# Routing inside the second 8-wide heads, a region of memory for each expert, and tiles read one by one

## The chip, the cores and the metric

The kernel runs on one core of a Trainium2 chip. The metric is the time of one execution in device microseconds, the median of the runs. The core has TensorE (matrix products, 128x128), VectorE and ScalarE (elementwise work), GpSimd (elementwise work, and transfers to rows given by an index), SyncE (SP, which issues the other transfers), an on-chip SBUF of 128 partitions, and eight PSUM banks. Engines run their own instruction streams in order and meet at semaphores.

## The reference, cut to what matters

Tokens are 32 sequences of 128, width 128, float32. Four layers follow each other, each an attention and a feed-forward part, both on a layer norm of `x` and added to `x`:

```python
x = x + _L2_xattn_ref(_layernorm(x), ctx, ctx, mask, ...)   # 16 heads of 8
x = x + _L2_ffn_ref(_layernorm(x), centroid, Wg, bg, W1, b1, W2, b2)
# _L2_ffn_ref, E = 8, K = 2, D = 128, H = 342
d2 = sum(xs * xs) + sum(centroid * centroid) - 2.0 * (xs @ centroid.T)
dist = sqrt(maximum(d2, 1e-12))
w, sel = top_k(dist, K)
w = softmax(w)
for e in range(E):
    h = silu(xs @ Wg[e] + bg[e]) * (xs @ W1[e] + b1[e])
    out = out + we[:, e:e + 1] * (h @ W2[e] + b2[e])
```

So each of the 4096 tokens goes to two of eight experts, 8192 rows in all. Layers 0, 1 and 3 are as they were.

## The kernel before

The program is a list of phases (attention and feed-forward of each layer). Each phase gives a function for each engine, and `barrier` at its end makes every engine wait for all five. The two phases here are `small_heads(2, ...)` (L280 on; the same maker also builds layer 0's heads) and `gated_experts` (L1707 on).

**small_heads.** B = 32 batches in NG = 8 groups of G = 4. A slot n = 4g + j is the attention of one batch, and in each slot TensorE makes scores of batch n+2, the turned scores and exponents' input of batch n (`turned`), and the values' product of batch n-1 (`attend`). The tile of scores `pair` holds half of the heads, so that VectorE takes two maxima a slot: `maximum(n+2, 0)`, then `normalise(n-1)`, then `maximum(n+2, 1)` and `split_max`. TensorE's `mask_scores` waits for a maximum to have read `pair`, and `turn_max` for `split_max`. Beside this, one PSUM bank M is used in turn by the group's other work: in slot j = 0 the queries of group g+1 (`project_q`), in j = 1 its values, in j = 2 the output of group g-1 (after which VectorE adds the residual and takes statistics), in j = 3 the transposes of group g+2 (`turn`) and at the slot's end its keys (`project_k`, copied by ScalarE's `evac_k`, its last instruction of the slot). VectorE's `moments(g-1)` is in slot 3 too. GpSimd runs a loop over g: for g >= 2 `residual(g)` (adds a constant row to x), then `rstd_of` group g-2 once `stats_ready` allows, then `masked(g+2)`, four multiplications that wait for the keys of group g+2. After the loop come the last two rstd. SyncE loads the context of each group, two groups ahead, once the values two groups back are made.

**gated_experts.** VectorE normalises all rows to `xn`; TensorE turns them and makes the distances' logits; VectorE chooses two experts per token for all 32 batches at once (`first_best` twice), TensorE counts with a triangular and a full matrix of ones, VectorE sums the counts over batches, and adds for each expert a base of full tiles: expert e's rows begin at a multiple of 128 behind those of the experts ahead. `where_i` holds each token's two rows. GpSimd scatters (L2100): for each batch and choice one indirect transfer of 128 rows of 130 words (128 values, the token's number, a code of the first choice) into the memory table `tokens_by_tile` of 72 tiles of 128 rows, which SyncE has filled with blanks (L1772, 8 transfers). When all 64 have landed, SyncE loads the 72 tiles in 8 transfers of 9 tiles (L1777). Then the tile loop: transpose (L1824), gate and up products (L1832, L1838), ScalarE copies the expert's weights (L1882) and applies the gate (L1889), VectorE multiplies (L2036) and copies (L2028, L2045), TensorE makes the down product (L1849) and GpSimd scatters the result (L2110). `places` on VectorE works out where the rows of 9 tiles go. SyncE reads the results back, ScalarE weighs them, and they are added to x.

## Time and profile before

| | us |
|---|---|
| median of 3 runs | 2105.51 |
| lowest and highest | 2103.83, 2106.74 |
| profiled execution | 2106.39 |
| span of its profile | 2104.5 |
| TensorE busy | 1760.6 (84%) |
| VectorE busy | 1061.4 (50%) |
| ScalarE busy | 912.2 (43%) |
| GpSimd busy | 665.5 (32%) |

The busy time is a sum over the whole span; a stage's own limit is read from a stretch of it. The second 8-wide heads run from about 920 to 1206 us from the span's start, the experts of layer 2 from there to about 1527. The profile counts waiting and the issue of transfers by SyncE as not busy.

### The profile page before, as it was taken

The page shows a single profiled execution, that of the slowest core. Times are in us where ns is not written, and L with a number is a line of the kernel's source. Part 1 is how long each engine was busy: PE and PEld are TensorE (multiplying, and loading weights), DVE is VectorE, ACT ScalarE, POOL GpSimd, SP SyncE. Part 2 cuts the span into 40 slices and gives each one's busy share as a digit, 9 for nine tenths or more (in the row PEclk, how much of TensorE's full clock was granted, in tenths as well). Part 3 has the DMA queues.
Part 4 walks back from the last instruction along what each step waited for, and adds up shares of the span by engine and source line. Part 5 has one row for each costly group of instructions (what it writes and reads, how often), then busy time and mean ns, then how long its engine had stood idle before and what let it go on. Part 6 is the DMA issues. An engine that isn't in the chain of part 4 may idle for free.

```text
span 2104.5 us, 47728 instructions
## 1 busy us (share of the span) xinstructions
PE 1760.6 (84%) x18872; PEld 1265.5 (60%) x18872; DVE 1061.4 (50%) x2947; ACT 912.2 (43%) x2497; POOL 665.5 (32%) x664
## 2 busy tenths in 40 slices
PE   6999984788489999979999740599369999999988
PEld 3555573666457877855565440599336666666763
DVE  4666546676432211234665540366635555555558
ACT  2333320676144444423333210377626566556635
POOL 3323202676211111121223117455612333332315
PEclk8999976888589999988999955799779999999979
DMA  5000001000000000020000021411310000000001
GB/s 168 7 13 7 2 2 25 16 11 1 6 1 2 2 2 1 1 94 14 8 12 3 17 89 52 121 32 32 90 57 6 1 7 6 6 6 1 2 1 41
DMA packets 45785, 50.76 MB, mean 24 GB/s; under 512 B 6858, under 2 KB 36453, under 8 KB 45309
## 3 DMA queue, kind: packets, MB, share of 16 engines
q1 hardware_dynamic: 41213, 39.19, 6.2%
q0 software_dynamic: 4352, 8.47, 1.3%
q8 instruction: 159, 2.61, 0.5%
q14 instruction: 61, 0.50, 0.1%
HBM read 32.29 MB, written 15.87 MB: 23 GB/s over the span
## 4 chain that ended last, share of the span: by engine, by line
PE 56%; issue 13%; DVE 5%; POOLq 4%; POOL 3%; DMA 1%; SPq 1%; ACT 1%; DVEq 1%; ACTq 0%
PE single L1520 5%; PE quad L1508 5%; PE pair L394 3%; PE single L445 3%; PE quad L1832 2%; PE single L1849 2%; PE quad L1838 2%; PE quad L422 2%; PE pair L2273 2%; PE pair L1467 2%; PE quad L2273 2%; PE single L2285 2%; PE quad L2250 1%; PE quad L2299 1%; PE single L2257 1%
## 5 line engine op out<-in xcount | busy, mean ns | idle before, releaser
L568 DVE TENSOR_REDUCE arena<-pair 128x8 f32<-128x1024 f32 x128 | 156.7, 1224 | 149.3 <-PE pair L394 146.9
L2506 POOL TENSOR_TENSOR arena<-arena 128x512 f32<-128x512 f32 x128 | 130.4, 1040 | 312.4 <-DVE arena L2429 312.4
L655 POOL TENSOR_SCALAR arena<-arena 128x512 f32<-128x512 f32 x56 | 86.7, 1565 | 307.8 <-ACT arena L500 307.8
L251 POOL TENSOR_TENSOR rstd<-var_eps,neg_half 128x4 f32<-128x4 f32 (+1 forms) x64 | 68.2, 1066 | 336.4 <-DVE var_eps L247 242.8
L548 ACT ACTIVATE arena<-quad 128x1024 f32<-128x1024 f32 x128 | 124.1, 1022 | 71.1 <-PE quad L428 71.1
L1578 ACT ACTIVATE arena<-quad,arena 128x256 f32<-128x256 f32 x256 | 110.7, 475 | 100.4 <-PE quad L1508 100.3
L394 PE MATMUL pair<-arena 32*128 32x512 f32 x512 | 147.3, 652 | 0.0
L2366 ACT ACTIVATE arena<-pair,arena 128x128 f32<-128x128 f32 x256 | 90.9, 380 | 91.4 <-DVE arena L2424 91.4
L1661 DVE TENSOR_TENSOR arena<-single,arena 128x512 f32<-128x512 f32 x32 | 22.1, 691 | 212.8 <-PE single L1520 212.8
L1508 PE MATMUL quad<-arena,wide 128*128 128x256 f32 x512 | 121.7, 385 | 4.7 <-issue 3.9
L1520 PE MATMUL single<-wide,arena 128*64 128x128 f32 x2048 | 123.9, 275 | 0.0
L2366 ACT ACTIVATE arena<-quad,arena 128x128 f32<-128x128 f32 x256 | 90.9, 381 | 75.9 <-DVE arena L2424 75.9
L1520 PEld LDWEIGHTS single<-wide,arena 128*64 128x64 f32 x2048 | 110.7, 137 | 15.9 <-issue 11.0
L1889 ACT ACTIVATE arena<-quad,arena 114x128 f32<-114x128 f32 x216 | 63.5, 364 | 119.3 <-PE quad L1832 118.1
L1508 PEld LDWEIGHTS quad<-arena,wide 128*128 128x128 f32 x512 | 93.3, 190 | 20.8 <-issue 8.7
L2110 POOL DMA_INDIRECT outputs_by_choice<-arena x72 | 71.0, 986 | 79.9 <-DVE arena L2045 65.2
L2036 DVE SCALAR_TENSOR_TENSOR arena<-quad,arena 114x128 f32<-114x128 f32 x216 | 62.4, 344 | 54.0 <-ACT arena L1889 43.1
L1824 PE MATMUL pair<-ident,arena 128*128 128x128 f32 x72 | 20.0, 281 | 82.9 <-DMA arena<-tokens_by_tile 82.9
L584 DVE RECIPROCAL arena<-single 128x128 f32<-128x128 f32 x64 | 61.3, 958 | 51.4 <-PE single L445 51.4
L1688 POOL TENSOR_TENSOR arena<-arena 128x512 f32<-128x512 f32 x32 | 34.8, 1097 | 164.8 <-DVE arena L1642 160.3
L445 PEld LDWEIGHTS single<-arena 128*32 128x32 f32 x2048 | 52.1, 109 | 48.4 <-issue 46.8
L2100 POOL DMA_INDIRECT tokens_by_tile<-arena x64 | 62.0, 969 | 59.3 <-DVEq L2002 40.1
(475 smaller groups left out, 4379.8 us busy)
## 6 DMA issues: line engine op xcount, KB each, us to landing
arena<-in_ctxT SPq DMA_DIRECT2D x32, 256.0 KB, 2.8
tokens_by_tile<-arena SPq DMA_DIRECT2D x8, 585.0 KB, 6.9
arena<-tokens_by_tile SPq DMA_DIRECT2D x8, 585.0 KB, 8.1
wide<-in_w SPq DMA_DIRECT2D x2, 2048.0 KB, 10.0
arena<-outputs_by_choice SPq DMA_DIRECT2D x16, 256.0 KB, 5.7
wide<-in_wgu SPq DMA_DIRECT2D x1, 2736.0 KB
x<-in_x SPq DMA_DIRECT2D x4, 512.0 KB, 7.2
out_x<-x SPq DMA_DIRECT2D x8, 256.0 KB, 2.3
```

Of the source, the lines that this page charges most:

```text
L394: mm = pe.matmul(S[:, r * 512:(r + 1) * 512], qT[g % 2][rows, j * P:(j + 1) * P], kv[g % 2][rows, j, :, :].rearrange("p a k -> p (a k)"), ...
L445: mm = pe.matmul(O[strip(c), k * P:(k + 1) * P], lhs(h), probs[m % 2][:, h, :], start=(a == 0), stop=(a == 3), skip_group_check=True)
L548: act.activation(probs[n % 2][:, 8 * p:8 * p + 8, :].rearrange("p h q -> p (h q)"), T[:, 1024 * p:1024 * p + 1024], ACT.Exp).then_inc(s["s ...
L568: dve.tensor_reduce(mx[m % 2][:, 8 * p:8 * p + 8], S[:].rearrange("p (h k) -> p h k", h=8), AX.X, ALU.max).then_inc(s["s_free"], 1)
L655: mm = pool.tensor_scalar(kv[g % 2][:, :, a, :], kf[g % 2], kmask[:, a:a + 1], None, ALU.mult)
L1508: pe.matmul(bank[2 + f][:, 0:G * K], w1[:, e, f * P:(f + 1) * P], exT[u][:, e, :], start=True, stop=True).then_inc(s["h_ready"], 1)
L1520: mm = pe.matmul(bank[6 + pair % 2][K * r:K * r + K, j * P:(j + 1) * P], h1T[e % 4][:, f, j * K:(j + 1) * K], w2[:, e, f, :], start=(f == ...
L1578: act.activation(h1T[e % 4][:, f, :], bank[2 + f][:, 0:G * K], ACT.Gelu_apprx_tanh, bias=b1c[:, e, f:f + 1]).then_inc(s["h_evac"], 1)
L2110: pool.indirect_dma_start(done, bass.IndirectOffsetOnAxis(ap=back_i[:, n:n + 1], axis=0), ysb[n % SLOTS], None, bounds_check=2 * B * P - 1 ...
L2273: mm = pe.matmul(S[o][:, r * 512 + i * P:r * 512 + (i + 1) * P], qT[g % 2][rows, 4 * o + i, j * P:(j + 1) * P], kT[g % 2][rows, 4 * o + i, ...
L2366: mm = act.activation(probs[t % 3][:, i, :], S[t % 2][:, i * P:(i + 1) * P], ACT.Exp, bias=minus_max[t % 3][:, i:i + 1], accum_out=total[t ...
L2506: pool.tensor_tensor(part, part, inv[t % 3][:, 4 * r:4 * r + 4].unsqueeze(2).broadcast_to([P, 4, P]), ALU.mult).then_inc(s["norm_ready"], 1)
```

## The change

Routing is done in units of two groups (UNIT = 8 batches). Units 0, 1 and 2 (batches 0 to 23) are routed inside `small_heads(2)`, unit 3 at the start of `gated_experts`.

In the heads: VectorE makes the normal rows of group g-1 in slot 3 of group g (`rows_normal`); TensorE turns them at the start of slot 0 of the next group (`turn_rows`, in bank M) and makes the logits behind `attend`, in an unused part of bank O; in the slots of groups 3, 5 and 7 VectorE chooses, sums and finds rows (`route`), with the count products behind `attend` in slot 2. `project_q` moves behind `attend` in slot 0. GpSimd builds the tables at its start, and scatters unit 0 in its pass g = 5, unit 1 in g = 7, unit 2 after its last rstd.

In memory each expert has a region of 4096 rows of its own (`tokens_by_expert`, 33,792 rows), so that a token's row no longer depends on how many tokens other experts get. The blanks, now 22 transfers of 12 x 128 rows, are written during the heads. In the experts a tile's first row is worked out on VectorE (`start_i`), read into a register by SyncE and loaded by a transfer of its own, up to eight ahead of the loop; `places` works on 4 tiles.

```diff
@@ program
-        fw_loads = {0: 3, 1: 3 + 1 + E + 1, 2: 1 + 2 + 1 + 1, 3: 2}
+        fw_loads = {0: 4, 1: 3 + 1 + E + 1, 2: 2 + 1 + 1, 3: 2}
...
+        REGION = B * P
+        FILL, FILLS = 12, (E * REGION + E * P) // (12 * P)
+        UNIT = 2 * G
+        by_tile = nc.dram_tensor("tokens_by_expert", [E * REGION + E * P, ROW], F32).ap()
...
+        def first_best(dve, values, chosen, top):
+            dve.tensor_reduce(top, values, AX.X, ALU.max)
+            dve.drain()
+            dve.tensor_tensor(key, values, along(top), ALU.is_equal)
...
+        def scatter(pool, k):
+            for n in range(k * UNIT, k * UNIT + UNIT):
+                for i in range(2):
+                    pool.indirect_dma_start(by_tile, bass.IndirectOffsetOnAxis(ap=where_i[:, i, n:n + 1], axis=0),
+                                            xr[:, n, :], None).then_inc(routed, 16)
@@ small_heads, sync
                 for g in range(2, NG):
                     load_ctx(sp, g)
+                    if l == 2 and g < 6:
+                        if g == 2:
+                            sp.wait_ge(blanked, 1)
+                        for i in range((g - 2) * 6, min((g - 1) * 6, FILLS)):
+                            sp.dma_start(by_tile[i * FILL * P:(i + 1) * FILL * P].rearrange("(p r) d -> p (r d)", p=P),
+                                         blank.rearrange("p r d -> p (r d)")).then_inc(blanked, 16)
@@ small_heads, tensor
+                def turn_rows(g):
+
+                    pe.wait_ge(s["xr_ready"], g + 1)
+                    pe.wait_ge(s["k_evac"], min(g + 4, NG))
+                    pe.wait_ge(s["x_done"], g + 1)
+                    for j in range(G):
+                        mm = pe.transpose(M[:, j * P:(j + 1) * P], xr[:, g * G + j, 0:P], ident[:])
+                    mm.then_inc(s["rt_ready"], 1)
...
+                    at, slot = divmod(m + 1, G)
+                    if routes(at) and at < NG and slot == 0:
+                        mm = logits(at - 2)
+                    if routes(at) and at % 2 == 1 and slot == 2:
+                        mm = counts((at - 3) // 2)
                     mm.then_inc(s["pv_ready"], 1)
...
-                    if j == 0 and g + 1 < NG:
+                    if j == 0 and routes(g):
+                        turn_rows(g - 2)
+                    if j == 0 and g + 1 < NG and l == 0:
                         project_q(g + 1, M)
...
                         attend(n - 1)
+                    if j == 0 and g + 1 < NG and l == 2:
+                        project_q(g + 1, M)
@@ small_heads, vector
+                def route(k, slot):
+                    if slot == 0:
+                        dve.drain()
+                        choose_first(dve, k)
+                    elif slot == 1:
+                        choose_second(dve, k).then_inc(s["sel_ready"], 1)
+                    elif slot == 2:
+                        sum_blocks(dve)
+                    else:
+                        find_rows(dve, k).then_inc(s["rows_ready"], 1)
+
+                def rows_normal(g):
+                    dve.wait_ge(s["rstd_ready"], g + 1)
+                    normal_rows(dve, g).then_inc(s["xr_ready"], 1)
...
                     if n + 2 < N:
                         maximum(n + 2, 0)
+                    if j == 3 and 1 <= g < NG - 1 and l == 2:
+                        rows_normal(g - 1)
                     if n >= 1:
                         normalise(n - 1)
                     if n + 2 < N:
                         maximum(n + 2, 1)
                         split_max(n + 2)
+                    if routes(g) and g % 2 == 1:
+                        route((g - 3) // 2, j)
@@ small_heads, gpsimd
                     if g >= 2:
                         residual(g)
                         pool.wait_ge(s["stats_ready"], g - 1)
-                        rstd_of(pool, (g - 2) * G)
+                        mm = rstd_of(pool, (g - 2) * G)
+                        if l == 2:
+                            mm.then_inc(s["rstd_ready"], 1)
                     if g + 2 < NG:
                         masked(g + 2)
+                    if l == 2 and g in (5, 7):
+                        pool.wait_ge(s["rows_ready"], (g - 3) // 2)
+                        if g == 5:
+                            pool.wait_ge(blanked, 1 + 16 * FILLS)
+                        scatter(pool, (g - 5) // 2)
                 for g in (NG - 2, NG - 1):
                     pool.wait_ge(s["stats_ready"], g + 1)
                     rstd_of(pool, g * G)
+                if l == 2:
+                    pool.wait_ge(s["rows_ready"], 3)
+                    scatter(pool, 2)
                 barrier(pool, phase)
@@ gated_experts, sync
-                sp.wait_ge(s["scattered"], 16 * 2 * B)
-                for i in range(LOADS):
-                    part = slice(i * PART, (i + 1) * PART)
-                    sp.dma_start(tokens[:, part, :], by_tile[i * PART * P:(i + 1) * PART * P]
-                                 .rearrange("(r p) d -> p r d", p=P)).then_inc(s[f"landed{i}"], 16)
+                sp.wait_ge(s["starts_ready"], 1)
+                sp.wait_ge(routed, 16 * 2 * B)
+                for n in range(TILES):
+                    if n >= LANES:
+                        sp.wait_ge(s["y_copied"], n - LANES + 1)
+                    row = sp.value_load(start_i[0:1, n:n + 1], min_val=0, max_val=E * REGION + E * P - P)
+                    sp.dma_start(tokens[:, n, :], by_tile[ds(row, P)]).then_inc(s[f"tile_in{n % LANES}"], 16)
@@ gated_experts, vector
-                for g in range(NG):
-                    for j in range(G):
-                        n = g * G + j
-                        mm = dve.tensor_scalar(xn[:, n, 0:P], x[:, n, :], mean[:, n:n + 1], rstd[:, n:n + 1],
-                                               ALU.subtract, ALU.mult)
-                    mm.then_inc(s["xn_ready"], 1)
-
+                for g in range(2):
+                    normal_rows(dve, 2 * K + g).then_inc(s["xr_ready"], 1)
...
+                choose_first(dve, K)
+                choose_second(dve, K).then_inc(s["sel_ready"], 1)
+                dve.wait_ge(s["counts_ready"], 1)
+                copy_counts(dve, count_bank)
+                sum_blocks(dve)
+                find_rows(dve, K).then_inc(s["rows_ready"], 1)
@@ gated_experts, gpsimd
-                pool.wait_ge(s["slots_ready"], 1)
-                pool.wait_ge(s["zeroed"], 1 + 16 * 8)
-                for n in range(B):
-                    for i in range(2):
-                        pool.indirect_dma_start(by_tile, bass.IndirectOffsetOnAxis(ap=where_i[:, i, n:n + 1], axis=0),
-                                                xn[:, n, :], None).then_inc(s["scattered"], 16)
+                pool.wait_ge(s["rows_ready"], 1)
+                scatter(pool, K)
```

`choose_first` has ten small operations (128x64 or 128x8), `choose_second` seven, `sum_blocks` eight, `find_rows` eight; `scatter` sixteen transfers.

## Rows read from the trace of the kernel before

**Rows 1.** Windows by stage: busy us (instructions), TensorE's clock, DMA share, GB/s.

```profile
920.00:1206.00 286.00, 261.69 (x4578) 154.83 (x4578) 163.97 (x332) 92.95 (x130) 66.33 (x49) 0.94 0.07 24
1206.00:1337.40 131.40, 25.16 (x114) 23.77 (x114) 25.80 (x90) 8.41 (x14) 65.33 (x76) 0.50 0.22 76
1337.40:1495.00 157.60, 154.65 (x1368) 153.26 (x1368) 96.65 (x388) 112.22 (x288) 83.83 (x80) 0.98 0.20 54
```

**Rows 2.** Timeline of GpSimd in the heads: start, duration, instruction, [idle before <-releaser].

```profile
1021.99 1.04 POOL L251 TENSOR_TENSOR rstd<-var_eps,neg_half 128x4 f32<-128x4 f32 x1
...
1109.25 6.19 POOL L655 TENSOR_SCALAR arena<-arena 128x512 f32<-128x512 f32 x4 [23.13 <-ACT arena L500]
...
1116.64 1.04 POOL L251 TENSOR_TENSOR rstd<-var_eps,neg_half 128x4 f32<-128x4 f32 x1
...
1166.93 1.02 POOL L251 TENSOR_TENSOR rstd<-var_eps,neg_half 128x4 f32<-128x4 f32 x1 [6.49 <-DVE var_eps L603]
...
1204.95 1.01 POOL L251 TENSOR_TENSOR rstd<-var_eps,neg_half 128x4 f32<-128x4 f32 x1 [9.37 <-DVE var_eps L603]
```

**Rows 3.** Timeline of VectorE, slots 1 to 3 of group 4.

```profile
1087.71 1.11 DVE L562 TENSOR_SCALAR arena<-x,mean,rstd 128x128 f32<-128x128 f32 x4
1090.36 1.22 DVE L568 TENSOR_REDUCE arena<-pair 128x8 f32<-128x1024 f32 x1 [1.54 <-PE pair L394]
...
1097.95 1.23 DVE L568 TENSOR_REDUCE arena<-pair 128x8 f32<-128x1024 f32 x1 [0.98 <-PE pair L394]
...
1103.60 0.16 DVE L603 TENSOR_SCALAR var_eps<-arena 128x4 f32<-128x4 f32 x1
1105.54 1.23 DVE L568 TENSOR_REDUCE arena<-pair 128x8 f32<-128x1024 f32 x1 [1.78 <-PE pair L394]
1107.44 0.96 DVE L584 RECIPROCAL arena<-single 128x128 f32<-128x128 f32 x1 [0.68 <-PE single L445]
...
1109.88 1.23 DVE L568 TENSOR_REDUCE arena<-pair 128x8 f32<-128x1024 f32 x1 [1.11 <-PE pair L394]
```

**Rows 4.** Timeline of TensorE: weight loads of an output, and a projection of queries.

```profile
1093.53 0.97 PEld L379 LDWEIGHTS single<-wo,arena 128*128 128x128 f32 x8 [0.76 <-issue]
...
1109.76 1.12 PE L361 MATMUL single<-arena,wq 128*128 128x512 f32 x2
```

**Rows 5.** Windows of 1 us for the clock, and two slots' ends on VectorE.

```profile
1203.00:1204.00 1.00, 0.00 (x0) 0.00 (x0) 0.91 (x5) 0.00 (x0) 0.00 (x0) 0.71 0.00 0
...
1343.00:1344.00 1.00, 1.00 (x9) 1.00 (x9) 0.10 (x1) 0.87 (x4) 0.00 (x0) 0.82 1.20 295
...
957.49 0.18 DVE L578 SCALAR_TENSOR_TENSOR arena<-arena 128x16 bf16<-128x16 f32 x1
...
967.40 0.18 DVE L578 SCALAR_TENSOR_TENSOR arena<-arena 128x16 bf16<-128x16 f32 x1
```

**Rows 6.** Timeline of the experts' front, all engines, and one scatter of results.

```profile
1206.04 9.07 DVE L1913 TENSOR_SCALAR arena<-x,mean,rstd 128x128 f32<-128x128 f32 x32 [1.17 <-POOLq L121]
...
1207.49 8.65 SPq L1772 DMA_DIRECT2D tokens_by_tile<-arena  x8
...
1215.21 1.71 PE L1805 MATMUL quad<-gate,arena 128*128 128x8 f32 x8
...
1216.78 1.09 PE L1792 MATMUL pair<-ident,arena 128*128 128x128 f32 x4
...
1242.65 0.20 DVE L1967 COPY arena<-arena 128x64 f32<-128x64 f32 x1
...
1250.02 1.67 POOL L2100 DMA_INDIRECT tokens_by_tile<-arena  x1 [40.11 <-DVEq L2002]
...
1330.25 0.96 POOL L2100 DMA_INDIRECT tokens_by_tile<-arena  x1 [0.30 <-issue]
1333.11 14.04 SPq L1777 DMA_DIRECT2D arena<-tokens_by_tile  x8
...
1345.76 0.99 POOL L2110 DMA_INDIRECT outputs_by_choice<-arena  x1 [14.55 <-DVE arena L2045]
```

357 lines of the change are left out of this document (216 added, 141 removed).

## The prediction

> **What bounds the kernel now.** I read first the busy time by stage [rows 1]. In the second 8-wide heads (920 to 1206) TensorE is busy 261.7 of 286 us at a granted clock of 0.94: a stage with almost no room. In the routing front of the experts (1206 to 1337.4) TensorE is busy 25 of 131.4 us and nothing is really computing: this is what the change attacks. In the tile loop (1337.4 to 1495) TensorE is busy 154.7 of 157.6 us, 2.19 us a tile for 72 tiles. Then I read the front as a timeline [rows 6]: normalised rows, transposes and logits, a choice on VectorE, and from 1250.02 to 1331.2 GpSimd issuing 64 scatters, one each 1.27 us, with nobody able to do anything useful. Last I read the heads' boundary between two groups on GpSimd [rows 2], VectorE [rows 3] and TensorE [rows 4], because the change puts new waits there.
>
> **Part 1, the front gets shorter.** Only the last unit of eight tiles is routed here. From the start of the stage (T): eight normal tiles at 9.07/32 = 0.28 us, the first four ready at T+1.2; transposes of a group 1.09 and its logits 1.71, all at the low clock as now [rows 6]. In TensorE's order (turn, turn, logits, logits), with ScalarE's copies beside it, that is done at T+2.3, 3.4, 5.2 and 6.9. VectorE then has 2 distance operations, 17 of the choice, the copy of the counts, 8 of the block sums and about 7 of the rows. A 128x64 operation takes 0.20 us and its successor starts some 0.08 later [rows 6]; with 0.28 a step, and pairs that overlap, distances and choice take 5.3, the count matmuls 1.1, the rest 3.6: rows known at T+17. Sixteen scatters at the spacing of [rows 6], (1330.25 - 1250.02)/63 = 1.27: 15 x 1.27 + 0.96 = 20.1, with 0.7 more for the slow first one: T+38. From the last scatter's end to the first reading transfer it takes 1.9 us now (1331.2 to 1333.11) and the first 585 KB block is usable 4.3 us later [rows 1, 6]; a tile of 65 KB behind a register read should take 2 to 4, I take 3: first tile at T+43. Against 131.4: **-88** (bounds -82 to -92). The tables of tile starts lie under the scatters.
>
> **Part 2, a scatter tail on the heads.** The third unit's rows are ready before the heads end, but GpSimd issues its 16 scatters after the last rstd. That rstd runs at 1204.95 to 1205.96 and the stage ends 0.08 later [rows 2, 6]. Now 20.1 to 20.8 us of scatters stand between, and all engines wait at the barrier: **+21** (20 to 23). Nothing hides it.
>
> **Part 3, the wait that decides.** VectorE gets in slot j = 3 of group g, for g = 1 to 6, between the first and the second maximum, `rows_normal(g-1)`, which waits for the rstd of group g-1. The statistics for it are ready early (1103.60 in [rows 3]). But GpSimd computes that rstd only in its pass g+1, behind `masked(g+2)`, and that waits for the keys that ScalarE copies at the very end of the same slot. In the trace it goes so [rows 2, 3]: the first maximum of the slot ends at 1106.77; masked starts at 1109.25 and takes 6.19; the rstd runs 1116.64 to 1117.68. Today nobody waits for it (there are five of this kind, the first at 1021.99). After the change VectorE stands from 1106.8 to 1117.7, then makes the four rows (1.11, as L562 in [rows 3]), the normalisation that it did from 1107.44 to about 1108.8 (1.35), and only then the second maximum (1.23), which ended at 1111.11: it will end at about 1121.5. TensorE's next score masks and the turned maxima wait for exactly this, and so does its new `turn_rows`. So each boundary gets 10.4 us longer, for g = 1 to 5: 52 us (9 to 11 each). For g = 6 there is no masked left and the rstd follows the statistics (as at 1166.93), so there it costs under 1 us.
> At g = 5 there is more: the first unit's 16 scatters are put behind masked(7) and ahead of pass 6, where the rstd is that VectorE wants. Queued behind them are residual(6) and this rstd; VectorE waits, and TensorE and ScalarE for it. +20.1 to 20.8. The second unit's scatters (pass 7) hold back only an rstd that no engine of the stage wants. **Together +73** (65 to 77).
>
> **Part 4, work inside the heads.** (a) project_q moves from the start of slot 0, where TensorE waits for the second maximum anyway, to behind attend: 1.12 [rows 4], now in the open, 7 times: +7.7 (5 to 8). `turn_rows` takes its old place in the shadow: nothing; if that cover is gone, 0.7 each. (b) Logits: 4 matmuls of 8 columns are bound by their weight loads, 0.97 for eight loads [rows 4], for 6 groups: +5.7 (4 to 7). Counts: 4 loads each, 3 times: +1.4. (c) VectorE: choose_first 10 x 0.28 = 2.8 against an idle time of 1.54 ahead of the next first maximum, choose_second 2.0 against 0.98 [rows 3]; of the excess about half a microsecond is hidden because TensorE needs that maximum later. About 1 us per odd group, three of them: +3 (0 to 8). Sums and rows fit in the longer idle times. (d) The setup (tables, row numbers, blank) lies beside the first loads: 0 (to +2).
> (e) The blank fill grows from 8 x 585 KB to 22 x 799 KB, 17.6 MB. The 8 old ones were issued in 8.65 us [rows 6] and landed at most some 8 us after, 4.7 MB in 17 us; six new ones are 4.8 MB in each group of 31.6 us. A context load is queued behind one batch and is needed more than a group (31.6 us) later: 0.
>
> **Part 5, the clock.** The clock of TensorE follows its work: when the heads' last matmuls are done it falls from 2.4 to 1.2 GHz (0.71 in 1203 to 1204, [rows 5]), and after the restart at 1337.4 it rises only in 1343 to 1344. At the start of the heads, where it is low for most of the time, a slot lasts from 957.49 to 967.40 [rows 5], 9.9 us, instead of the 7.6 from one first maximum to the next [rows 3]. Each of the five stalls has some 9 us without a matmul, so each should be followed by one slot at the low clock: 5 x 2.5 = **+12** (3 to 25). TensorE: Matmul & The Clock Gate (What's actually happening, in the Trainium skill) says the throttled state is the default and activity releases it; the rows agree. If a stall of this kind left the clock up, the sum would be 12 less.
>
> **Part 6, the tile loop.** 72 single loads, each behind a register read, eight in flight. The 8 big loads took 14.04 us in all [rows 6], 0.2 us a tile if it is descriptors, 1.8 a load if it is by instruction: both below 2.19, so the queue keeps up. `places` every 4 tiles instead of every 9 is 10 more rounds of 0.75 us on an engine with a third of its time free: 0 (to +6).
>
> **Sum.** -88 + 21 + 73 + 7.7 + 5.7 + 1.4 + 3 + 12 = +36. The profiled execution took 2106.4 (span 2104.5 and 1.9 outside), 0.9 above the median of 2105.5: 2106.4 + 36 = 2142. All terms at their low ends give about +5, at their high ends +70.
>
> **Rivals.**
> 1. The wait costs little, because VectorE's and GpSimd's order overlap other than I read, or TensorE's buffers cover it. Then Part 3 and Part 5 fall away and the time is 2106.4 - 88 + 21 + 18 = 2057, faster. For it speaks that the front's 88 us are sure; against it that the two maxima and the rstd are in strict order on their engines, and that TensorE has a depth of one slot only. The deciding point: from about 2.5 us per boundary (plus the scatters) upward the change is no longer faster than 1%; at 3 us less per boundary than I say it is still slower. Chance 0.12.
> 2. The wait costs half: if attend and the keys shift earlier within the slot, or the g = 5 scatters find the needed rstd done. 2142 - 36 = 2106, within a few us of no change. Chance 0.06.
> 3. The 72 loads do not keep up, since a load with a register's row costs the queue 2.5 us or more: 72 x 0.4 = +29 on my sum, 2171. No row shows such a load. Chance 0.08.
> 4. Scatters are slowed by VectorE's work beside them. In this trace a scatter beside a busy VectorE in the tile loop takes as long to issue as in the quiet front (0.99 against 0.96, [rows 6]). As a mechanism here: the second unit's scatters begin after 1168 in old time [rows 2] and have 38 us before the last rstd, 2.4 us each; were each issued in three times its 0.96, with the 0.3 between, they would take 51 and push the tail out by 13: 2155. SBUF — State Buffer (Who interferes with whom, in the Trainium skill) has it that GpSimd is shut out of writing descriptors while VectorE runs a two-port operation; that is the rule behind this rival, and the row of the tile loop speaks against its size here. Chance 0.04.
> 5. The forecast: both waits as computed. Chance 0.70, with 2125 to 2170 as its own range.
>
> **Numbers.** A measurement can tell about 0.2% (4 us) from no change. Faster: rival 1 and a third of rival 2: 0.14. Within 0.2%: 0.03. Slower: 0.83. The range reaches from 2104, the low ends of all terms and half of rival 2, to 2176, the high ends and rival 3.
>
> **What would show it.** In the profile after: VectorE idle about 11 us ahead of the new row operation in slot 3, released by GpSimd's rstd, four times, and 31 us once; TensorE idle 9 us at the same places, its clock at 0.5 after them; sixteen scatters of 20 us between the last rstd and the next stage; 43 us from there to the first tile's transpose; an unchanged 157 us for the tiles. The heads' stage, 286 us now, should take about 286 + 103 + 21 = 410. What would make the prediction wrong: less than 370 there (the wait is not what I read), or more than 165 for the tiles.

## The result, and the profile after

The changed kernel took 2178.1 us (median of 4, 2175.4 to 2179.8) against 2105.0 of the kernel before beside it: ratio 1.0346, interval 1.0328 to 1.0364. The prediction had the side right (slower) and the size wrong: +73 us, not +36, and 2 us outside its range. One thing from the experiments belongs here: on another chip the same kernel took 2140.2 us (e5), 2 us from the predicted 2142, and on a third 2168.6 (e9). The kernel before took 2101 to 2105 on all of them.

Windows of the profile after, in the order heads, scatter tail, front, tile loop (to be held against [rows 1]):

```profile
921.20:1329.30 408.10, 303.34 (x4664) 181.00 (x4664) 183.40 (x457) 96.63 (x137) 99.95 (x87) 0.81 0.18 65
...
1329.30:1353.50 24.20, 0.00 (x0) 0.00 (x0) 0.01 (x1) 0.00 (x0) 15.44 (x16) 0.50 0.13 44
1353.50:1395.40 41.90, 9.09 (x40) 8.23 (x40) 15.05 (x65) 4.44 (x6) 17.58 (x22) 0.50 0.09 28
1395.40:1562.00 166.60, 157.45 (x1368) 153.58 (x1368) 100.87 (x414) 111.08 (x287) 82.67 (x78) 0.98 0.21 56
```

The front is 42 us in place of 131, the tail 24. The heads are at 408 in place of 286, at a mean clock of 0.81 in place of 0.94. The tile loop is 9 us longer.

VectorE in the heads, every instruction of it that stood long (timeline; the bracket is the idle time before it and who ended it):

```profile
1024.76 1.12 DVE L327 TENSOR_SCALAR arena<-x,mean,rstd 128x128 f32<-128x128 f32 x4 [10.93 <-POOL rstd L262]
...
1069.91 1.11 DVE L327 TENSOR_SCALAR arena<-x,mean,rstd 128x128 f32<-128x128 f32 x4 [10.94 <-POOL rstd L262]
...
1115.99 1.11 DVE L327 TENSOR_SCALAR arena<-x,mean,rstd 128x128 f32<-128x128 f32 x4 [10.90 <-POOL rstd L262]
...
1163.21 1.12 DVE L327 TENSOR_SCALAR arena<-x,mean,rstd 128x128 f32<-128x128 f32 x4 [10.94 <-POOL rstd L262]
...
1232.81 1.12 DVE L327 TENSOR_SCALAR arena<-x,mean,rstd 128x128 f32<-128x128 f32 x4 [31.43 <-POOL rstd L262]
...
1287.46 0.96 DVE L782 RECIPROCAL arena<-single 128x128 f32<-128x128 f32 x1 [19.35 <-remote]
```

The first five are the waits of Part 3, four of 10.9 us and one of 31.4: they end at exactly the rstd that [rows 2] showed behind masked. The sixth was not foreseen. VectorE waits there for pv_ready, which is TensorE's, but the profile finds no TensorE instruction that ends then and says "remote". What GpSimd, TensorE and ScalarE did at that time:

```profile
1264.17 1.02 POOL L262 TENSOR_TENSOR rstd<-var_eps,neg_half 128x4 f32<-128x4 f32 x1 [6.48 <-DVE var_eps L822]
...
1265.37 1.03 POOL L415 DMA_INDIRECT tokens_by_expert<-arena  x1 [0.18 <-issue]
...
1271.51 3.12 PE L568 MATMUL pair<-arena 32*128 32x512 f32 x4
...
1284.43 0.96 POOL L415 DMA_INDIRECT tokens_by_expert<-arena  x1 [0.31 <-issue]
...
1288.29 0.60 ACT L711 ACTIVATE arena<-single 128x512 f32<-128x512 f32 x1 [21.40 <-remote]
...
1289.97 0.63 PE L155 MATMUL pair<-maskS2own,identb 64*64 64x512 bf16 x1 [11.78 <-DVE arena L766]
```

From 1265.37 to 1285.39 GpSimd issues the 16 scatters of scatter(1), which no engine of the stage waits for. Four matmuls of L568 last 3.12 us instead of 1.08, and TensorE's signals reach VectorE and ScalarE only 2 us after the last scatter. The products that VectorE waits for (L619) are on record until 1270.1, 17 us before it goes on. From about 1278 TensorE itself waits, for the maximum that VectorE can only take after that. So the halt, as I call it, has two parts: TensorE's instructions come slowly, and their signals come late.

### The profile page after: what moved, and what is told of

Read it like the earlier page. It is cut to its first block, busy times and chain, and to the rows that moved or that the text cites. A ratio compares the mean times of both kernels' runs of the same rounds, so it can differ in the third digit from the quotient of the medians.

```text
span 2178.1 us, 48570 instructions
## 1 busy us (share of the span) xinstructions
PE 1791.6 (82%) x18884; PEld 1276.6 (59%) x18884; DVE 1077.5 (49%) x3087; ACT 911.6 (42%) x2496; POOL 666.3 (31%) x664
## 4 chain that ended last, share of the span: by engine, by line
PE 54%; issue 10%; DVE 7%; POOL 6%; POOLq 4%; DVEq 2%; DMA 1%; ACT 1%; another core or an unknown queue 1%; SPq 1%; ACTq 0%
PE single L1778 5%; PE quad L1766 5%; PE single L2076 2%; PE quad L2059 2%; PE quad L2065 2%; PE pair L568 2%; PE single L619 2%; PE pair L2434 2%; POOL tokens_by_expert L415 2%; PE pair L1725 2%; PE quad L2434 2%; PE single L2446 2%; POOLq L132 1%; PE quad L2411 1%; PE quad L596 1%
## 5 line engine op out<-in xcount | busy, mean ns | idle before, releaser
L568 PE MATMUL pair<-arena 32*128 32x512 f32 x512 | 153.5, 673 | 0.0
L619 PEld LDWEIGHTS single<-arena 128*32 128x32 f32 x2048 | 53.8, 112 | 51.8 <-issue 43.1
L596 PE MATMUL quad<-arena 32*128 32x128 f32 x2048 | 83.3, 304 | 0.0
L715 ACT ACTIVATE arena<-single 128x128 bf16<-128x128 bf16 x64 | 17.8, 278 | 154.9 <-PE single L580 154.9
```

What stands on the lines that cost most here:

```text
L568: mm = pe.matmul(S[:, r * 512:(r + 1) * 512], qT[g % 2][rows, j * P:(j + 1) * P], kv[g % 2][rows, j, :, :].rearrange("p a k -> p (a k)"), ...
L596: pe.matmul(T[:, r * 512 + a * P:r * 512 + (a + 1) * P], kv[g % 2][strip(r), j, a, :], qT[g % 2][strip(r), j * P:(j + 1) * P], start=False ...
L619: mm = pe.matmul(O[strip(c), k * P:(k + 1) * P], lhs(h), probs[m % 2][:, h, :], start=(a == 0), stop=(a == 3), skip_group_check=True)
```

## Experiments

The runs fell on four chips, called W, X, Y and Z here; that of the first measurement isn't recorded. Runs that are compared stood on the same chip unless it is said.

**e1 (chip W): the wait alone taken away.** In the second heads GpSimd's order is changed, nothing else:

```diff
-                    if g >= 2:
+                    if g >= 2 and l == 0:
                         residual(g)
                         pool.wait_ge(s["stats_ready"], g - 1)
-                        mm = rstd_of(pool, (g - 2) * G)
-                        if l == 2:
-                            mm.then_inc(s["rstd_ready"], 1)
+                        rstd_of(pool, (g - 2) * G)
+                    if 1 <= g < NG - 1 and l == 2:
+                        residual(g + 1)
+                        pool.wait_ge(s["stats_ready"], g)
+                        rstd_of(pool, (g - 1) * G).then_inc(s["rstd_ready"], 1)
                     if g + 2 < NG:
                         masked(g + 2)
```

> The changed kernel with one edit: in the second 8-wide heads GpSimd runs residual(g + 1) and rstd(g - 1) before masked(g + 2), not behind it. Everything else is computed as before. Theory of the wait (the prediction's): the five waits of VectorE for rstd of 10.9 us each and the sixth of 31.4 us go, since rstd(g - 1) needs only the statistics of the same slot; 54.7 + 31.4 = 86 us leave the stage and some of TensorE's clock comes back, so 2085 to 2095 us. Rival (a scatter halts TensorE by itself): scatter(1) stood beside TensorE's work for 19 to 21 us in the changed kernel without being waited for. Then scatter(0), which now also runs beside TensorE's work, costs its 20 us again, and the time is 2105 to 2115 us. In both the group periods of groups 2 to 4 fall from 45 to 47 us to 33 to 36 us.

Measured: 2064.0 us, ratio to the kernel before 0.9811 (0.9777 to 0.9845). The wait is gone; of e1 the rstd on GpSimd, and the rows on VectorE right behind the first maximum:

```profile
1045.40 1.04 POOL L262 TENSOR_TENSOR rstd<-var_eps,neg_half 128x4 f32<-128x4 f32 x1 [6.47 <-DVE var_eps L822]
```

```profile
1047.10 1.23 DVE L766 TENSOR_REDUCE arena<-pair 128x8 f32<-128x1024 f32 x1 [1.78 <-PE pair L568]
1048.24 1.11 DVE L327 TENSOR_SCALAR arena<-x,mean,rstd 128x128 f32<-128x128 f32 x4
```

It is 21 us below the low end of what I expected, and both bursts of scatters ran beside TensorE's work (1160.67 to 1180.85 and 1184.55 to 1204.53) with no halt. So either the halt needed the wait, or it hung on something outside the program. The expectation was counted from the 2178 of another chip; e5 shows what it should have been counted from.

**e2, e3 (chip W): scatters alone.** The kernel before with 16 scatters of its own behind masked(6), and with plain transfers of the same bytes in their place:

```diff
+                    if l == 2 and g == 4:
+                        for i in range(16):
+                            pool.indirect_dma_start(extra_rows, bass.IndirectOffsetOnAxis(ap=extra_at[:, i:i + 1],
+                                                    axis=0), extra, None).then_inc(extra_done, 16)
```

```diff
+                            pool.dma_start(extra_rows[i * P:(i + 1) * P], extra).then_inc(extra_done, 16)
```

> The kernel before with 16 indirect scatters added in the second 8-wide heads, on GpSimd right behind masked(6), one behind the other: each writes a blank tile of 128 rows of 520 bytes to a DRAM tensor of its own, at row numbers set at the start. Nothing reads it and GpSimd has no consumer that is late by its 20 us there. If scatters only cost the time of GpSimd: no change, 2105 us within 3. If a burst of scatters halts TensorE by itself: 15 to 21 us more, 2120 to 2126 us, with VectorE waiting for TensorE in one stretch of the burst's length.

> As the previous one, with 16 plain transfers from GpSimd's queue in the place of the indirect scatters: same tile, same bytes. If it is the bytes or the queue that halts TensorE, the time rises as there (15 to 21 us); if it is the indirect form, in which GpSimd works out the descriptors, it stays at 2105 us within 3.

Measured: 2103.0 (0.9996, 0.9980 to 1.0011) and 2104.8 (0.9996, 0.9980 to 1.0012), ten runs each: nothing, on this chip.

**e5, e6, e7, e8 (chip X).** e5 is the changed kernel untouched.

> The changed kernel, unchanged, on the chip of the other runs of this call. Asked: is the halt of 19 us at scatter(1) (VectorE and ScalarE waiting for semaphores of TensorE that came only when the last scatter had landed), and the hitch at every eighth tile of the tile loop, in this kernel's every run, or in some executions or chips only? If it belongs to the kernel: 2178 us within 5, with a wait of about 19 us ahead of RECIPROCAL and a tile loop of 161 us between first and last transpose. If it belongs to the chip or the execution: without the halt and with a tile loop of 149 us, 2140 to 2150 us.

Measured: 2140.2 (2137.3 to 2143.4), ratio 1.0175 (1.0140 to 1.0210). Its five waits are there (10.92, 10.94, 10.89, 10.93 and 31.37), the halt isn't. Windows of e5: the heads, the 23 us at scatter(1), tail, front, tile loop:

```profile
919.00:1300.30 381.30, 293.07 (x4664) 175.36 (x4664) 187.72 (x457) 96.63 (x137) 99.14 (x87) 0.83 0.19 70
1259.70:1282.90 23.20, 21.71 (x419) 13.35 (x411) 15.38 (x35) 6.97 (x9) 16.39 (x17) 1.00 0.16 49
1300.30:1324.50 24.20, 0.00 (x0) 0.00 (x0) 0.05 (x1) 0.00 (x0) 15.38 (x16) 0.50 0.13 44
1324.50:1366.30 41.80, 9.09 (x40) 8.23 (x40) 14.99 (x65) 4.44 (x6) 17.54 (x22) 0.50 0.09 28
1366.30:1522.00 155.70, 153.95 (x1368) 153.31 (x1368) 100.67 (x417) 112.15 (x288) 83.29 (x79) 0.98 0.22 60
```

and the same 23 us behind rstd(5) in the profile after:

```profile
1264.20:1287.40 23.20, 11.34 (x124) 5.06 (x116) 2.25 (x5) 1.94 (x2) 16.44 (x17) 0.65 0.14 48
```

GpSimd did the same (16.4 us in 17 instructions), the transfers moved the same (49 GB/s in e5, 48 in the profile after). TensorE began 419 matmuls in e5 and 124 in the profile after.

e6 moves scatter(0) only:

```diff
-                    if l == 2 and g in (5, 7):
-                        pool.wait_ge(s["rows_ready"], (g - 3) // 2)
-                        if g == 5:
+                    if l == 2 and g in (6, 7):
+                        pool.wait_ge(s["rows_ready"], g - 5)
+                        if g == 6:
                             pool.wait_ge(blanked, 1 + 16 * FILLS)
-                        scatter(pool, (g - 5) // 2)
+                        scatter(pool, g - 6)
```

> The changed kernel with scatter(0) moved from behind masked(7) to behind rstd(4), one step of GpSimd's order later; nothing else differs, so the five waits of 10.9 us stay. Theory of the wait: the wait of 31.4 us in group 5 becomes one of 10.9 like the others, so 20 to 21 us less than the changed kernel run beside it. Rival (a burst of scatters beside TensorE's work halts it): the 20 us come back as a halt during scatter(0), and the time is that of the changed kernel within 4 us.

Measured: 2123.7 (1.0088, 1.0054 to 1.0121), 16.5 less than e5, where 20 to 21 were expected; the fifth wait is like the others:

```profile
1214.61 1.12 DVE L327 TENSOR_SCALAR arena<-x,mean,rstd 128x128 f32<-128x128 f32 x4 [10.93 <-POOL rstd L262]
```

The heads are 22.2 us shorter (table below). So a scatter(0) behind which nobody is queued costs nothing on this chip, and ahead of the rstd it costs its whole length.

e7 is e1 with the third unit's scatters out of the tail:

```diff
-                if l == 2:
-                    pool.wait_ge(s["rows_ready"], 3)
-                    scatter(pool, 2)
...
+                scatter(pool, 2)
                 pool.wait_ge(s["rows_ready"], 1)
                 scatter(pool, K)
```

> The changed kernel with rstd(g - 1) ahead of masked(g + 2), as in e1, and scatter(2) moved from the stage's tail to the start of the experts' stage, in which GpSimd otherwise has nothing to do until the rows of the last unit are known, 16.6 us after the stage begins. The tail of 20 us goes, and scatter(2) + scatter(3) end at 2 x 20.2 us + some 2 us behind the stage's start, not at 16.6 + 20.2: 20 - 5 = 15 to 17 us less than e1's 2064, so 2046 to 2050 us. Rival: VectorE's small operations of the front are slowed by GpSimd's scatters beside them, so that the rows come later than 20 us behind the start: a gain of 10 us or less, 2054 or more.

Measured: 2044.1, ratio 0.9709 (0.9676 to 0.9741), 2 us below what was expected. Tail and front together are one window of 50.1 us, where e5 has 24.2 + 41.8:

```profile
1224.40:1274.50 50.10, 9.09 (x40) 8.23 (x40) 15.43 (x65) 4.44 (x6) 32.45 (x38) 0.50 0.14 44
```

e8 is the kernel before with project_q and its evacuation behind attend:

```diff
-                    if j == 0 and g + 1 < NG:
+                    if j == 0 and g + 1 < NG and l == 0:
                         project_q(g + 1, M)
...
                         attend(n - 1)
+                    if j == 0 and g + 1 < NG and l == 2:
+                        project_q(g + 1, M)
```

> The kernel before with one part of the change alone: in the second 8-wide heads project_q(g + 1) and its evacuation stand behind attend, not at the slot's start. My prediction gave this 7.7 us in all (7 groups x 1.1 us), because its eviction then stands where TensorE has to wait for it. If it is so: 2111 to 2113 us. Rival (ScalarE and the bank are free anyway): no change, 2105 within 3.

Measured: 2109.0, ratio 1.0021 (1.0003 to 1.0039), 6 us above the kernel before beside it by the medians and 4 by the ratio: between the two times expected. The trace is sharper. From one masked to the next on GpSimd, in e8:

```profile
1047.14 6.19 POOL L659 TENSOR_SCALAR arena<-arena 128x512 f32<-128x512 f32 x4 [24.18 <-ACT arena L502]
...
1079.75 6.19 POOL L659 TENSOR_SCALAR arena<-arena 128x512 f32<-128x512 f32 x4 [24.17 <-ACT arena L502]
```

32.61 us a group, against 31.55 in the kernel before (1077.70 to 1109.25, the second in [rows 2]): 1.06 us for each of 7 projections, 7.4.

**e9, e10, e11 (chip Y): the same programs again.**

> The changed kernel, unchanged, once more, on a chip that may be another one. It took 2178 us where it was first measured and 2140 us beside e6 to e8; the 38 us between them are the halts of TensorE beside bursts of scatters (22 us at scatter(1), 12 us in the tile loop). If the halts hang on the chip, this is near one of the two, 2140 or 2178, within 4 us in all of its runs; if they hang on the execution, its runs spread between the two.

> The kernel of e7, unchanged (rstd ahead, scatter(2) in the experts' front), beside the changed kernel. Without halts 2044 us as in e7. With them, if every burst beside TensorE's work halts it: scatter(0) and scatter(1) cost 20 us each and the tile loop 12, so 2095 us; if only what the changed kernel does at scatter(1) brings it about, 2056 us (the tile loop alone).

> The kernel of e2, unchanged (the kernel before with 16 scatters of its own beside TensorE's work), beside the changed kernel. On a chip without halts: 2105 us, as in e2. Where the changed kernel shows the halt: 2120 to 2126 us if a burst of scatters is enough for it, 2105 us if it needs something of the changed kernel.

Measured: the changed kernel 2168.6 (1.0312, 1.0290 to 1.0334), e7's kernel 2088.4 (0.9929, 0.9906 to 0.9952), the kernel before with 16 scatters 2121.9 (two runs, 1.0100, 1.0080 to 1.0121). The first lies between the two expected values, 9 us under the 2178 of the first chip, with 162.1 us of tiles instead of 168.6; the second is 7 under the 2095 of a halt at both bursts. The runs of the changed kernel lie together on each chip (2175 to 2180, 2137 to 2143, 2162 to 2169), so the halt isn't drawn anew at each execution. This chip has it, and in the heads a burst of scatters is all that the kernel before needs to show it: +21 us, where e2, byte for byte the same program, showed nothing. Of e11, TensorE in the burst:

```profile
1112.64 1.25 POOL L701 DMA_INDIRECT extra_rows<-arena  x1 [0.19 <-issue]
...
1118.15 0.51 PE L432 MATMUL quad<-arena 32*128 32x128 bf16 x8
...
1119.82 0.26 PE L432 MATMUL quad<-arena 32*128 32x128 bf16 x4 [1.15 <-issue]
...
1130.47 0.37 PE L449 MATMUL single<-arena 128*32 128x128 f32 x1 [1.04 <-issue]
...
1131.86 0.96 POOL L701 DMA_INDIRECT extra_rows<-arena  x1 [0.31 <-issue]
...
1135.44 1.94 ACT L552 ACTIVATE arena<-quad 128x1024 f32<-128x1024 f32 x2 [17.90 <-remote]
1135.50 1.23 DVE L572 TENSOR_REDUCE arena<-pair 128x8 f32<-128x1024 f32 x1 [17.53 <-remote]
```

and of e2 the same instructions in the same burst:

```profile
1121.11 0.40 PE L432 MATMUL quad<-arena 32*128 32x128 bf16 x16
...
1121.72 1.94 ACT L552 ACTIVATE arena<-quad 128x1024 f32<-128x1024 f32 x2 [1.21 <-PE quad L432]
1122.35 0.81 PEld L449 LDWEIGHTS single<-arena 128*32 128x32 f32 x32 [0.76 <-issue]
```

In e11 TensorE gets through one to four matmuls and then waits for "issue", that is for nothing that the profile shows; the 16 matmuls of L432 that took 0.40 us in e2 are spread over more than 3 us. GpSimd issues one scatter each 1.26 us in both. TensorE doesn't wait for VectorE or ScalarE there; they wait for it, for signals that come 11 to 14 us after the products on record (L432 until 1121.5, L398 until 1124.8). SBUF — State Buffer (Who interferes with whom, in the Trainium skill) says that "PE and ACT never wait on anyone" and that only the port pair of VectorE and GpSimd is contended. e2 agrees, e11 doesn't: its 17.5 us decide for that chip. Whether TensorE waits for SBUF there or for something else, no run shows.

Small bursts halt too. In the tile loop root() (L2267) holds GpSimd for 1.7 us at every eighth tile, after which three result scatters follow each other. The profile after:

```profile
1487.91 1.04 POOL L2271 DMA_INDIRECT outputs_by_choice<-arena  x1 [0.18 <-issue]
...
1489.26 0.99 POOL L2271 DMA_INDIRECT outputs_by_choice<-arena  x1 [0.30 <-issue]
...
1490.55 0.98 POOL L2271 DMA_INDIRECT outputs_by_choice<-arena  x1 [0.30 <-issue]
...
1492.33 0.88 ACT L2112 ACTIVATE arena<-quad,arena 114x128 f32<-114x128 f32 x3 [2.76 <-PE quad L2059]
```

and e5, on chip X:

```profile
1489.02 0.99 POOL L2271 DMA_INDIRECT outputs_by_choice<-arena  x1 [0.30 <-issue]
...
1490.31 0.98 POOL L2271 DMA_INDIRECT outputs_by_choice<-arena  x1 [0.30 <-issue]
...
1491.64 0.88 ACT L2112 ACTIVATE arena<-quad,arena 114x128 f32<-114x128 f32 x3 [0.55 <-PE quad L2059]
```

Same burst, ScalarE's idle time 2.76 against 0.55. In the profile after, seven such pairs of tiles take about 5.9 us instead of 4.2, 12 us in all.

**Stages side by side**, us, from the timelines (heads: ScalarE's first instruction of the stage to the start of the last rstd; then to the first tile's transpose; then to the last result scatter):

```
                        heads   to tile 1   tiles   median of the run
before                  282.4     132.5     157.3   2105.0  (first chip)
after                   405.9      67.2     168.6   2178.1  (first chip)
e16, before + burst     277.1     133.2     155.6   2102.5  (X)
e5, changed             379.9      67.1     156.2   2140.2  (X)
e6, scatter(0) later    357.7      67.3     155.9   2123.7  (X)
e7, both edits          298.8      51.2     156.3   2044.1  (X)
e2, before + burst      277.9     133.1     156.0   2103.0  (W)
e1, rstd ahead          296.1      67.5     155.7   2064.0  (W)
e11, before + burst     295.2     133.1     156.7   2121.9  (Y)
e9, changed             405.7      67.1     162.1   2168.6  (Y)
e10, e7's kernel        341.5      52.3     162.6   2088.4  (Y)
```

The first slots of the heads differ by up to 5 us from run to run (277.1 to 282.6 for unchanged heads), so a difference of that size in the first column says nothing. The later slots repeat closely: from one RECIPROCAL of VectorE to the next a slot of the unchanged heads takes 7.59 us, or 8.8 at the end of a group, in e3, e12 and e16 alike. Where few us matter I go by slots below.

**e4 (chip W): pairs, in the wrong place.** e7's kernel, but with the scatters of units 0 and 1 two at a time, one pair in each slot of groups 4 to 7:

```diff
+                        for j in range(G):
+                            if g >= 4:
+                                pool.wait_ge(s["pv_ready"], g * G + j)
+                                scatter_one(pool, (g - 4) * G + j)
+                            if j == 2 and 1 <= g < NG - 1:
+                                residual(g + 1)
```

> The changed kernel with rstd(g - 1) ahead of masked(g + 2), as in e1, the scatters of units 0 and 1 issued two at a time, one pair in each slot of groups 4 to 7 (GpSimd waits for the slot's pv_ready), and those of unit 2 moved from the stage's tail into the start of the experts' stage, where GpSimd has 16 us of idle time. Theory of the wait with scatters that cost nothing while GpSimd is on time: 2178 - 86 (waits) - 20 (the halt at scatter(1)) - 17 (tail) - some clock = 2050 to 2060 us, faster than the kernel before. Rival (each scatter halts TensorE for its own 1.27 us, paced or not): 32 x 1.27 = 40 us stay in the stage, 2090 to 2100 us.

Measured: 2071.8 (0.9844, 0.9813 to 0.9874): neither of the two. In slot 3 the pair's own wait for pv_ready stands ahead of the rstd:

```profile
1119.38 2.53 DVE L327 TENSOR_SCALAR arena<-x,mean,rstd 128x128 f32<-128x128 f32 x4 [4.28 <-POOL rstd L262]
```

It is the mistake of the changed kernel in small: 4.3 us of wait, and rows that take 2.53 instead of 1.11 (e1), where GpSimd's masked (from 1119.34) now runs beside them. SBUF — State Buffer (Who interferes with whom, in the Trainium skill) has the port pair that VectorE and GpSimd share as an exclusive lock. That would explain the second; no run here takes it apart.

**e12 to e15 (chip Z), e16 to e18 (chip X): what of the burst does it.** e12 and e17 are e3's kernel, e16 is e2's. e13 issues e2's 16 scatters singly, each behind its own wait:

```diff
+                    if l == 2 and g in (5, 6):
+                        for i in range((g - 5) * 8, (g - 4) * 8):
+                            pool.wait_ge(s["s_ready"], 45 + i)
```

e14 and e15 are e7 with singles and with pairs, both with the slot's rstd first and with root() in sixteen smaller pieces (`n % 4 == 2`); e18 is e15 again. Of e15 (e14 waits for `s_ready` ahead of each scatter instead):

```diff
+                            if j == 3 and 1 <= g < NG - 1:
+                                pool.wait_ge(s["stats_ready"], g)
+                                rstd_of(pool, (g - 1) * G).then_inc(s["rstd_ready"], 1)
+                            if g >= 4:
+                                pool.wait_ge(s["pv_ready"], g * G + j)
+                                for i in range(2):
+                                    scatter_one(pool, (g - 4) * G + j, i)
```

> The kernel of e3, unchanged: the kernel before with 16 plain transfers from GpSimd's queue behind masked(6). On a chip with halts, 16 indirect scatters there cost 21 us (e11). If the bytes or the queue do it: 2117 us or more. If it is the indirect form: 2101 us within 4. On a chip without halts it tells nothing new (2105).

> The kernel before with the 16 indirect scatters of e2 and e11, but spaced: eight in each of two groups, each behind its own wait for s_ready, some 4 us apart, so that one has landed before the next is issued. If the halt comes of scatters that follow each other without a gap: 2101 us within 4 also on a chip with halts. If each scatter halts TensorE for its own time: 2117 us or more, as in e11.

> The changed kernel with rstd(g - 1) ahead of masked(g + 2), scatter(2) in the experts' front as in e7, the scatters of units 0 and 1 issued singly (each behind its own s_ready, some 4 us apart, from group 4 to 7) and behind rstd in slot 3, and root() in sixteen pieces of 4 columns in place of eight of 8, so that no burst of y scatters follows it. If spacing removes the halt: 2040 to 2050 us on any chip (e7's 2044 without halts, 2088 with). If not: 2044 and 2088 to 2095 us. If the scatters put ahead of GpSimd's other work make rstd late as in e4: 2055 to 2065 us.

> As e14 with the scatters in pairs, one pair in each slot behind pv_ready. If a gap of 5 us behind each pair is enough: the time of e14 within 4 us. If the second scatter of each pair halts TensorE for its 1.3 us on a chip with halts: 16 x 1.3 = 20 us more than e14.

> The kernel of e2 and e11 (16 indirect scatters without a gap, in the kernel before), as a control: 2121 us if this chip halts, 2104 within 4 if it doesn't.

> The kernel of e3 and e12 (16 plain transfers of the same bytes from GpSimd's queue). If the indirect form is what halts: 2104 us within 4 also where e16 is at 2121. If the bytes or the queue are: e16's time within 4.

> The kernel of e15 (rstd ahead, scatter(2) in the experts' front, units 0 and 1 in pairs, one pair a slot behind pv_ready, smaller root pieces). If pairs escape the halt: 2045 to 2055 us on any chip, where e7's bursts took 2044 without and 2088 with halts. If they only escaped because the chip of e15 had none: 2065 us or more where e16 is at 2121.

Measured on Z: e12 2106.2 (1.0019, 1.0001 to 1.0038), e13 2111.0 (1.0035, 1.0016 to 1.0054), e14 2058.9 (0.9788, 0.9745 to 0.9830), e15 2052.2 (0.9752, 0.9718 to 0.9787). Measured on X: e16 2102.5 (1.0004), e17 2103.8 (1.0005), e18 2042.1 (0.9715, 0.9686 to 0.9745).

X has no halt, as the control e16 shows, so e17 says nothing of its cause. Z has it, and the traces of Z show it in three places.

First, the tile loop has its hitches (in e12 tiles of 2.59, 2.81 and 2.35 us, as in e11; on X none over 2.3 but two at the start). Second, the experts' front of e14 and e15 has a burst of 32 scatters, of units 2 and 3. Of e15 there, VectorE and ScalarE:

```profile
1256.94 0.76 DVE L2176 TENSOR_TENSOR arena<-arena 128x576 f32<-128x576 f32 x1 [2.58 <-issue]
...
1276.59 0.53 ACT L2106 ACTIVATE arena<-quad 114x432 f32<-114x432 f32 x1 [42.47 <-remote]
```

and of e18, the same program on X, the same ScalarE instruction:

```profile
1251.99 0.53 ACT L2106 ACTIVATE arena<-quad 114x432 f32<-114x432 f32 x1 [22.46 <-PE quad L2051]
```

So the halt is not TensorE's alone. A row of small operations of VectorE (L2171 to L2192 of e15) takes 5.1 us from first start to last in e18 and e7 on X, 15.6 in e15 and 12.6 in e14 on Z, and 11.4 in e10 on Y, with idle times for "issue" in between. It costs little there, since the tiles wait for the scatters anyway. Third, the last five scatters of e14's heads follow each other without a gap, because the value that they wait for is capped, and there TensorE halts:

```profile
1216.63 0.33 PE L605 MATMUL quad<-arena 32*128 32x128 bf16 x9
...
1218.96 0.96 POOL L413 DMA_INDIRECT tokens_by_expert<-arena  x1 [0.30 <-issue]
...
1221.08 0.26 PE L605 MATMUL quad<-arena 32*128 32x128 bf16 x1 [1.19 <-issue]
```

That slot takes 13.7 us from one RECIPROCAL to the next, where e15 has 7.25.

With that, e12 and e15 have an answer, for Z. The plain transfers of e12 leave the heads as they were (277.9, the same as e3 on W), and the slots beside them stay at 7.59 us; its median is 4 us above the kernel before by the ratio, not 17 or more:

```profile
1109.29 8.84 POOL L701 DMA_DIRECT2D extra_rows<-arena  x16
...
1114.45 0.40 PE L432 MATMUL quad<-arena 32*128 32x128 bf16 x16
```

They go through the same queue (software_dynamic), with the same 512 packets and 1.07 MB as the 16 scatters of e11. So on Z neither the queue nor the packets nor the bytes are enough; what is left is the indirect form. (The plain ones are issued in 8.8 us instead of 20; but e14's halt stands beside five scatters in 6 us.) And pairs escape (the time is 7 us below e14's, where it was expected within 4): the heads of e15 take 298.2 us with 16 pairs in them, those of e18 on X 299.0, while the burst in e15's own front halts. The smaller pieces of root() don't escape altogether: they leave five tiles of 2.4 to 2.5 us in e15, and its tiles take 158.8 against 155.6 in e18.

Singles are less clear. The heads of e13 take 286.4 us against 277.9 in e12, and its slots say where: 4.8 of the 8.4 us are one slot, in which a VectorE operation (L580) takes 1.22 us instead of 0.17 beside GpSimd's residual and TensorE's granted clock is then 0.50 (1174 to 1183). That is no halt, and no wait in these heads ends with "remote". The other slots beside scatters are longer by 0.1 to 0.9, and why is open. e14's time lies in the third of its ranges, but not by that range's mechanism: its heads take 311.0, the end of the burst above costs 6.5 of the 12.8 more than e15, and no VectorE wait for rstd is among them. Neither e13 nor e14 ran on a chip without halts.

## Why the prediction was wrong, and where it was right

**Where there is no halt it held, by its own terms.** On chip X (e5 against e16): heads +102.8, predicted 73 + 7.7 + 5.7 + 1.4 + 3 + 12 = 102.8; tail and front -66.1, predicted -88 + 21 = -67; tiles +0.6, predicted 0. Sum +37.3; the medians differ by 37.4 (2140.2 - 2102.8, the kernel before beside e5). To the tenth this is chance: e16's first slots were among the short ones. By slots, from the fourth on, the heads of e5 are 97.6 longer than those of e12, and nearly all of the 5 between is the first slots.
- Part 1: 41.8 to 41.9 us from the stage's start to the first tile, predicted 43. Right.
- Part 2: 24.2, predicted 21. The 16 scatters took 20.0 us (1329.45 to 1349.46); behind them GpSimd stood another 4.1 at the barrier, where in the kernel before the next stage began 0.1 behind the rstd [rows 2, 6]. Low by 3.
- Part 3: four waits of 10.9 and one of 31.4, 75.1 us in the profile after, predicted 73. I counted five waits of 10.4 and added the scatter to the fifth, which is what happened. e1 and e7 show that they are the cause: the heads fall by 81.1 us (e5 to e7), waits and lost clock together, predicted 85. With that rivals 1 and 2 are out.
- Part 4: what is left of the heads without the waits is e7 - e16 = +21.7 us (e1 - e2: +18.2; by slots, e7 against e12, 16.2), predicted 17.8. project_q alone is 7.4 by the group's length in e8, predicted 7.7.
- Part 5: the slots right behind the five waits take 9.9, 9.6, 12.1, 12.4 and 10.2 us in e5, and 9.5, 9.5, 9.3, 9.5 and 9.5 in e7, without waits: 6.9 us, predicted 12. Too high by 5: behind the first two waits it is 0.4 and 0.1, not 2.5, though the granted clock was 0.50 behind the first (e5, 1020.8 to 1027).
- Part 6: the loads keep up; rival 3 is out (156.2 in e5 against 157.3). So is rival 4: the scatters beside VectorE's work are 1.26 us apart, as in the quiet tail.
- The high ends of all terms, as they are written, add up to +75, which is 2182, and not to +70: the "(to +6)" of Part 6 is missing from that sum. The stated 2176 was 6 us too low by its own terms. That 2178 would lie within 2182 would not have made the mechanism right.

**The step that failed is a sentence of Part 3: "The second unit's scatters (pass 7) hold back only an rstd that no engine of the stage wants."** It is true of GpSimd's queue, and the 16 scatters were priced by it alone. On chips with the halt they stop TensorE too: heads 405.9 and 405.7 us against 379.9, +26. (By slots, in the profile after against e5: 27.3, 12.2 and 8.8 us in place of 7.9, 8.4 and 7.6, 24.5 in all.) Rival 4 asked whether VectorE would slow the scatters and not whether the scatters would slow TensorE. The second failure is Part 6's "0 (to +6)": 168.6 against 156.2, +12.4, by the same cause behind root(). 26 + 12.4 = 38.4; the measured excess over the forecast is 36 (2178 - 2142), over e5 38. The kernel before has nearly none of it, because its 64 scatters stand in the front, where TensorE has nothing to do: I read that row [rows 6] as waste only. It had two longer tiles in its tile loop on the first chip, 2.52 and 2.77 us instead of 2.09. I know of no other sign before the result, and the prediction doesn't use it.

**Shown and not shown.** Shown: in the heads a burst of indirect scatters alone is enough (e11), the same program is free of it on other chips (e2, e16), plain transfers of the same bytes and pairs of scatters don't bring it about on a chip that has it (e12, e15), and the five waits cost what was predicted (e1, e6, e7). Not shown: what stops. The transfers themselves go at the same rate with and without (48 and 49 GB/s), so they aren't slowed. VectorE is held up as well (e15's front), so the cause isn't in TensorE alone. Instructions and signals both come late, and no run separates the two. TensorE's instructions come in transfers too (in the profile's queue "instruction" 2 packets on q8 in the halt of the profile after, 3 in e5); whether the scatters hold these up is a rival that nothing here tests. Nor is it shown how long a burst must be: the slow instructions begin 2 us behind the first scatter in the profile after, 5 to 6 in e11, 15 in e15's front, and the front of the profile after, with 16 scatters, shows nothing. Nor is it shown that the chip itself is the condition and not, say, the hour: X had no halt at two times, each other chip was met once.

**A version that beats both:** e7 (rstd ahead of masked, third scatter in the front) is at 0.9709 on X and at 0.9929 on Y, where the halts take back 44 us. With pairs in the slots (e15, e18) it is at 0.9752 on Z, which has the halts, and 0.9715 on X. It didn't run on Y.

## What to carry to other kernels

A consumer that is added in the middle of a slot has to be followed back through its producer's whole queue: here GpSimd's rstd moved ahead of masked, together with the third scatter moved out of the tail, turns 1.0175 into 0.9709. Price moved transfers for every engine that works beside them, not only for the queue that issues them: work that looks like waste in a quiet stage may be cheap because the stage is quiet. Where indirect scatters have to stand beside busy engines, issue them in pairs with other work between (e15). And when a result is off by a round block, run the unchanged kernel once more elsewhere before explaining it.

## What was not expected of the hardware

- A burst of 16 indirect scatters, 1.26 us apart, halts TensorE for 17 to 22 us on some chips (e11: VectorE's wait of 17.53; profile after: 19.35; e10: +42.7 us of heads for two bursts against e7) and not at all on others (e2, e16). Three in a row are enough for 1.7 us (profile after, tile loop). Sixteen plain transfers of the same bytes through the same queue (e12) and sixteen pairs (e15) left the heads alone on a chip that shows it.
- VectorE is held up too: 5.1 us of small operations took 15.6 beside the burst in e15's front.
- In the halt TensorE's instructions are still recorded, some at their places, while their signals come later, 11 to 17 us in the heads (e11, profile after), with the releaser "remote". In these two stages "remote" ends waits in the profile after, e9, e10, e11, e14 and e15, and in no trace of W or X. In a program of one core it is worth a look at what the DMA-issuing engines do.
- VectorE's four row operations took 2.53 us beside GpSimd's masked (e4) and 1.11 alone (e1).
- Behind 16 scatters GpSimd stood 4.1 us at the barrier (profile after), behind an rstd 0.1 (kernel before).
